# Transposing new rows between two halves of the projected keys, and masking 61 text columns instead of 77, in a fused four-part kernel

## The reference

```python
q = _heads(x @ Wq)                       # 16 heads of 64
k = _heads(ctx_t @ Wk)                   # 77 text columns
v = _heads(ctx_t @ Wv)
sim = jnp.einsum('bihd,bjhd->bhij', q, k) * SCALE
dist = jnp.clip(jnp.arange(TEXT)[None, :] - jnp.arange(nq)[:, None], -MAXREL, MAXREL) + MAXREL
k2 = rel_k[dist]                         # MAXREL = 16
sim = sim + jnp.einsum('bihd,ijd->bhij', q, k2) * SCALE
attn = jax.nn.softmax(sim, axis=-1)
out = jnp.einsum('bhij,bjhd->bihd', attn, v)
out = out + jnp.einsum('bhij,ijd->bihd', attn, rel_v[dist])
```

## Time and profile before

| what | us |
|---|---|
| three runs | 971.49, 966.97, 970.35; median 970.35 |
| the profiled execution, its own time | 968.65 |
| its span (first to last instruction) | 966.7 |
| PE busy in the span | 863.4 (89%) |
| DVE, ACT, POOL busy | 600.0, 467.1, 391.7 |
| mean granted TensorE clock | 0.971 of full |
| steps 1 to 15 of the second attention | from about 544 to 848 |
| a pair of steps in the loop (671.66 to 711.23) | 39.57 |

### The profile page before, as it was taken

The page is one execution under the profiler, slowest core; times in us unless marked ns, Lnnn a source line. Parts: engine busy times, 40 slices in busy tenths (PEclk is TensorE's granted clock), DMA queues, the critical chain, the costliest instruction groups (busy, mean ns, idle before and its releaser), DMA issues. The chain is left out here.

```text
span 966.7 us, 26667 instructions
## 1 busy us (share of the span) xinstructions
PE 863.4 (89%) x9044; PEld 729.9 (76%) x9045; DVE 600.0 (62%) x1484; ACT 467.1 (48%) x1194; POOL 391.7 (41%) x610
## 2 busy tenths in 40 slices
PE   4888888759999999998999899999999999779995
PEld 3676776439999999996556588888888887667784
DVE  3587887545555555542027567868668787459995
ACT  3788787412222222222343354445444454459895
POOL 4478886620000000006102346445564545436662
PEclk9999999979999999999999999999999999889998
DMA  6454656342433333316864696777676875212111
GB/s 165 118 164 155 196 159 214 136 165 76 137 95 93 108 95 98 98 35 211 287 197 148 144 180 151 157 148 167 142 158 143 163 157 119 64 41 63 58 59 45
DMA packets 190187, 128.27 MB, mean 133 GB/s; under 512 B 128544, under 2 KB 175648, under 8 KB 189984
## 3 DMA queue, kind: packets, MB, share of 16 engines
q1 hardware_dynamic: 155728, 93.72, 37.5%
q10 hardware_dynamic: 31312, 25.17, 9.1%
q0 software_dynamic: 3072, 8.39, 2.7%
HBM read 78.25 MB, written 48.99 MB: 132 GB/s over the span
## 5 line engine op out<-in xcount | busy, mean ns | idle before, releaser
L1745 ACT ACTIVATE c_pT<-c_T 128x512 f32<-128x512 f32 (+2 forms) x90 | 50.2, 595 | 104.9 <-PE c_T L1904 74.0
L1689 POOL TENSOR_TENSOR c_soft<-c_soft,c_share 128x616 f32<-128x616 f32 (+2 forms) x96 | 70.5, 764 | 63.3 <-DVE c_share L2158 61.8
L1699 POOL MEMSET d_round<- 128x1 f32 x1 | 0.1, 99 | 227.4 <-POOLq L970 227.4
L1080 ACT ACTIVATE b_rowsT<-b_RT 128x256 f32<-128x256 f32 x39 | 15.0, 385 | 157.8 <-PE b_RT L1122 157.8
L1194 DVE COPY b_w<-moe_w 128x1024 f32 x78 | 53.6, 688 | 53.0 <-issue 47.5
L1131 PEld LDWEIGHTS b_G<-b_rowsT,b_w 128*128 128x128 f32 x624 | 77.2, 195 | 4.5 <-DVE b_w L1194 2.4
L1131 PE MATMUL b_G<-b_rowsT,b_w 128*128 128x128 f32 x624 | 77.9, 279 | 1.7 <-DVE b_w L1194 1.1
L1208 DVE SCALAR_TENSOR_TENSOR b_hidT<-b_U,b_bias,b_gate 128x128 f32<-128x128 f32 x156 | 43.9, 344 | 55.6 <-PE b_U L1131 55.6
L1131 PE MATMUL b_U<-b_rowsT,b_w 128*128 128x128 f32 x624 | 76.8, 277 | 0.0
L1158 PE MATMUL b_Y<-moe_w,b_hidT 128*128 x312 | 73.9, 380 | 1.0 <-DVE b_out L1239 1.0
L1131 PEld LDWEIGHTS b_U<-b_rowsT,b_w 128*128 128x128 f32 x624 | 73.6, 194 | 0.0
(11 more groups left out here) (241 smaller groups left out, 2073.1 us busy)
## 6 DMA issues: line engine op xcount, KB each, us to landing
moe_w<-in_L_Wl SPq DMA_DIRECT2D x16, 512.0 KB
rel_windows<-c_relw ACTq DMA_DIRECT2D x28, 276.0 KB, 5.6
c_bias<-rel_windows SPq DMA_DIRECT2D x16, 462.0 KB, 4.9
prob_rows<-c_soft SPq DMA_DIRECT2D x16, 462.0 KB, 5.4
early<-in_L_early SPq DMA_DIRECT2D x16, 384.0 KB, 3.2
values<-c_pT ACTq DMA_DIRECT2D x22, 256.0 KB, 2.6
b_rows<-expert_lists SPq DMA_DIRECT2D x39, 128.0 KB, 2.2
expert_out<-b_out SPq DMA_DIRECT2D x39, 128.0 KB, 1.7
```

Source lines behind the costliest of these rows:

```text
L1689: ins = nc.gpsimd.tensor_tensor(soft[p][:, hs, a:z], soft[p][:, hs, a:z], share[:, s, hs].unsqueeze(2).to_broadcast([P, HS, z - a]), ALU.mult)
L1745: nc.scalar.activation(dst, view(T[k]), ACT.Copy, **kw).then_inc(g["emptied"], 1)
```

## The change

It has two parts. In odd steps, PE transposes the new rows after the second of the four key groups, and no longer before the last quarter of the weighted sum; ACT's list follows (its first exponential is now ahead of the key groups, its copy to `xT` between the second and the third). The far tails are multiplied and summed over columns 16 to 76 only, 61 instead of 77. `TEXT` is 77 and `MAXREL` 16.

```diff
-        far = sb("c_far", [P, NH, TEXT])
+        far = sb("c_far", [P, NH, TEXT - MAXREL])
...
-                nc.gpsimd.tensor_tensor(far[:, :, :], soft[p][:, :, 0:TEXT],
-                                        cst("behind_band").unsqueeze(1).to_broadcast([P, NH, TEXT]), ALU.mult).then_inc(g["tails"], 1)
+                nc.gpsimd.tensor_tensor(far[:, :, :], soft[p][:, :, MAXREL:TEXT],
+                                        cst("behind_band")[:, MAXREL:].unsqueeze(1).to_broadcast([P, NH, TEXT - MAXREL]), ALU.mult).then_inc(g["tails"], 1)
...
-                if there(b + 2):
+                if p == 0 and there(b + 2):
                     rows()
                 if not first:
                     exps(b, p, 0)
                 if p == 1 and there(b + 2):
                     projected(kT, PAIR_TILES[:2])
+                    rows()
                     exps(b, p, 1)
                     projected(kT, PAIR_TILES[2:])
                     queries(p, two)
...
-            def projected(weight):
-
-                for first_tile, end in PAIR_TILES:
+            def projected(weight, tiles):
+
+                for first_tile, end in tiles:
...
-                if there(b + 2):
+                if p == 0 and there(b + 2):
                     n_rows = rows(b + 2, p)
                 if not first:
                     attend(b - 1, i - 1 + p, 1 - p, n, (3,))
                 if p == 1 and there(b + 2):
                     context(i + 1)
-                    projected(wk[0])
+                    projected(wk[0], PAIR_TILES[:2])
+                    n_rows = rows(b + 2, p)
+                    projected(wk[0], PAIR_TILES[2:])
```

More of the change, by code:

```diff
@@ L2043, in _ @@
             context(0)
-            projected(wk[0])
+            projected(wk[0], PAIR_TILES)
             pe.wait_ge(g["emptied"], TURNS_AHEAD - 2 * (len(VALUE_TILES) - FIRST_TILES))
```

## The result

The changed kernel took 963.79 us (median of 20 runs, 958.43 to 968.55), the kernel before 968.74 (20 runs, 964.44 to 974.43). The ratio is 0.9944, with a 95% interval of 0.9927 to 0.9962: 5.4 us less, and between 3.7 and 7.1. The profiled execution's span is 962.8 us, 3.9 less.

What follows compares the result with a forecast made beforehand. PE, busy 89% of the span, loses time waiting for `xn` in odd steps. Gains of 2.4 + 0.5 + 0.4 + 0.2 = 3.5 us give 965.15 (profiled) or 966.85 (median); predicted 966.0, range 962.5 to 970.

Steps and rivals of the forecast that it cites:

- likeliest case: Whole kernel: the main forecast, 3.5 us less, own range 2.5 to 4.5 us, 964 to 968; chance 0.55.
- first rival: Step 1: PE's clock holds after its shorter pause, 1.55 us more won, 5.1 us in all, 963.6 to 965.3; chance 0.17.
- faster by over 0.5%: Whole kernel: the first two rivals and a share of the forecast's upper edge; chance 0.29.
- The move gives little by itself: Step 7: moving the transposes gives at most 0.16 us; a 0.35 bank pause and a wait for ACT replace the `xn` wait.
- The tails pull the whole chain: Odd steps: narrower `tails` take 0.475 us less, bringing L2145, `xn`, `less_max`, exponential and third key copy 0.47 earlier.
- 0.6 us for such a step: Steps 5, 7, 9, 11: queries start at 676.30 against 676.93 in step 7; 4 x 0.6 = 2.4 us.
- The sum L2164: Step 7, DVE: shortening it from 1.40 to 1.11 buys nothing, since `xn` also waits for POOL's L1678.
- Steps 3 and 13: PE's waits there less the 0.35 us bank pause: 0.5 us gained in step 3, 0.4 in step 13.
- Step 1: PE stands still 2.6 us instead of 3.1, the clock falls again during the queries; net gain 0.2 us.
- The end: Steps 14 and 15 prepare no rows and `tails` is off the path there: 0 gained.
- Slower by short pauses: Steps 3 to 13: rival where short bank-turn pauses lower PE's clock, 974.5 to 976.2 us; chance 0.05.

Runs made afterwards that it cites:

- the fill that doesn't read: Kernel before with the far tails left out: GpSimd multiplies one column and fills two buffers with constants; a pair took 38.46 us, single execution 964.85 us.
- the subtraction from PSUM: Kernel before with 61-column tails; scores plus bias written back to PSUM, maximum and subtraction read there; 38.28 us a pair, ratio 0.9904.
- all tails late: Kernel before with 61-column tails issued one step later, behind the inverse deviation, their sum behind the second `less_max`; 41.43 us a pair, ratio 1.0202.
- all tails late and the transposes moved: Changed kernel with its tails issued one step later, behind the inverse deviation; 41.31 us a pair, ratio 1.0147.
- both places tried here: 61-column tails one step later behind the inverse deviation (ratio 1.0202), or only even tiles' behind the gather (1.0075), against the kernel before.

## Why the prediction was right

The forecast was 966.0 us in 962.5 to 970, a gain of 3.5 us; measured were 963.79 and 5.4 us (3.7 to 7.1). In the loop the chain of causes held, and the sizes were too small. The number by itself speaks less well for the forecast: 963.79 lies just below the likeliest case's own 964 to 968 and inside the first rival's 963.6 to 965.3, and "faster by over 0.5%", which is what was measured (0.56%), had a chance of 0.29. It is the profiled execution that decides between the two: in step 1 its clock fell, as forecast, and the loop gave more.

- **The move gives little by itself.** Forecast at most 0.16 us in step 7, with waits of 0.35 for the bank and one for ScalarE. Shown by the move alone: 0.13 a pair, waits of 0.30 and 0.67.
- **The tails pull the whole chain.** Forecast 0.475 less for `tails` (measured 2.37 to 1.89) and as much for the subtraction (2.33 to 1.85). Right, and the cause is shown by the fill that doesn't read and by the subtraction from PSUM.
- **The term "0.6 us for such a step" was mis-sized**, about 0.8 a pair. Measured against PE's output projection, in step 7: the subtraction's end came 0.49 earlier, `xn` 0.59, the exponential 0.67, the queries 0.82 (14.72 to 13.90). Two small terms were set to nothing. The sum L2164 I had called hidden (it shrinks with `far`, so VectorE's list is the same in its order but not in this width): `xn` had waited for it, since with the shorter one `xn` follows the inverse deviation's start by 0.61 and not 0.70. The same 0.1 removed the wait in even steps, which I had left out; in the two kernels here that still sum 77 columns (the move alone, and the tails left out) it stays at 0.15 to 0.17. And the exponential, which I had read as released by the subtraction, had stood behind ScalarE's own second key copy, which ended at 675.46; afterwards it waits for the subtraction alone. The last 0.15 is the slack between the third key copy and the queries, which I had seen. A restart of 0.11 (queries 3.84 us instead of 3.73) goes off again.
- **Steps 3 and 13.** Forecast 0.5 and 0.4; with the even steps beside them 0.69 and 0.47.
- **Step 1.** Forecast a pause of 2.6 and a fall of the clock, net 0.2. Measured a pause of 2.43, a fall to 0.50, net 0.24. The rival in which the clock holds is not dead, though: in the move-only kernel the pause at this place was 2.23, the queries took 3.81 and the clock held, and with all tails late and the transposes moved it held after 2.44 (3.81 again). Nor is 0.24 sure to be the move's worth here: to step 2's queries the traces with unmoved transposes took 31.7 to 34.2 us (36.8 with all tails late), those with the transposes between the key halves 30.5 to 32.6 (33.6).
- **The end.** Forecast 0. A wait that I hadn't counted on absorbed what the clock gave: in step 14 the clock stayed high in this execution, and step 15 then stood still for 3.05 us instead of 1.39 ahead of the transposes of the band. Its load from memory had been issued at 819.69, 3.3 us before they began; that they waited for it I infer, since the bracket names no releaser.
- **Slower by short pauses** didn't happen: in the loops of the change, the move alone and the moved kernel with the subtraction from PSUM, the granted clock stayed at 1.00 with pauses of 0.3 us. (By its own measure this rival was mis-added: four falls come to 4 x 1.55 - 3.5 = 2.7 us, and six are needed for 4.85.)

**What stays open.** The timed median fell by 4.95 us and the ratio says 5.4, the traces show 4.4 in this stage. The last part of the kernel, which the change doesn't touch, took 122.3 to 126.8 us in the traces here, from the last output projection to the end, with no order among kernels, and step 1 took 13.4 to 18.8 to its queries. One profile of each can't say whether the missing 0.5 to 1 us is a gain in step 1 that comes in some executions only; the interval holds 4.4 as well.

## What to carry to other kernels

When a wait is taken away by reordering one engine, follow the next thing that this engine shares with its supplier: here the copy that frees the bank hung on the same late VectorE chain, so the wait changed its name and kept most of its length. Look for an operation that takes far longer in one step than in another; here a neighbour's work was in it, and shortening that neighbour by 20%, with the sum behind it, was worth five times the reordering. Moving such a neighbour needs a place where nothing that matters reads beside it, and both places tried here cost time; making the hurt operation immune (one operand from PSUM) was worth more than either.

## What the hardware showed that I had not expected

- A VectorE `tensor_scalar` on 128x256 with its two scalars in memory, 0.41 us alone, takes 1.98 beside a reading GpSimd product. It isn't only two-tensor operations that are held up.
- GpSimd can be the one that is held up. In step 15 of the kernel before the subtraction began first, at 818.05, and took 0.81 us; `tails` began at 818.28 and took 2.79 instead of 2.37.
- A reading GpSimd product may hold VectorE up before its own record begins: the subtraction began at 676.92 by the record, the product at 677.50, behind a gather, and the subtraction still took 3.15 us and ended 0.68 after the product, much like the 0.65 of the kernel before. It isn't the gather, beside which the same subtraction takes 0.80 in the changed kernel (671.97, the gather from 671.58 to 672.53). The profile's own note calls GpSimd's spans rough, so whether the product really began earlier isn't shown; but the order of the two records doesn't tell who waits.
- The length of one pause of PE doesn't tell whether the clock falls. In step 1, 2.43 us was followed by a fall, but 2.23, 2.44 and, with the transposes one quarter later, 2.94 by none. 1.84 in step 14 was followed by one in the kernel before and by none after the change. Of the pauses of 1.6 us for `xn` in the loops with all tails late one in each was followed by a fall, a granted clock of about 0.57 for some 4 us; those are the two pairs that took 1.6 us more.
